# Layer 1 of a two-layer decoder: one pipeline over sequences in place of a loop over groups of four

## What is computed

```python
x = layernorm(x + L0_attn(x)); x = layernorm(x + L0_xattn(x, ctx)); x = layernorm(x + L0_ffn(x))
# layer 1, self-attention: 16 heads of 32, one chunk of 128 tokens
q, k, v = rotary(x @ Wq), rotary(x @ Wk), x @ Wv
y = rms_norm(((q @ k.T) * decay) @ v) @ Wo
x = layernorm(x + y)
# layer 1, cross attention: 8 heads; a token holds 16 features of a head; the 512 columns attend to one another
qk = einsum('bhdq,bhdl->bhql', x, ctx) / sqrt(16)          # 512 x 512 for each head
x = layernorm(x + gamma * einsum('bhql,bhdl->bhdq', softmax(qk), ctx))
x = layernorm(x + experts(x))
```

## Time and profile before

| | us |
|---|---|
| median of three runs (3161.3 to 3161.7) | 3161.61 |
| the profiled execution | 3157.47 |
| its span, first to last instruction | 3155.6 |
| mean granted TensorE clock | 0.925 |

### The profile page before, as it was taken

One profiled execution on the slowest core, in us unless ns is written; L12 is line 12 of the kernel. 1 busy time (PEld: TensorE's weight loads), 2 busy tenths in 40 slices (PEclk: granted clock), 3 DMA queues, 4 the chain that ended last, 5 costly groups with the idle time before them and its releaser, 6 DMA issues. The chain is left out here.

```text
span 3155.6 us, 35463 instructions
## 1 busy us (share of the span) xinstructions
PE 2751.0 (87%) x11005; PEld 1378.1 (44%) x11006; DVE 1416.2 (45%) x2531; ACT 931.9 (30%) x1937; POOL 522.7 (17%) x524
## 2 busy tenths in 40 slices
PE   7999999999998567778778778785989999999998
PEld 3545544554554334224223223223535655566543
DVE  4545635564563522664663673671412222222245
ACT  2334424333433421362362353353001111111101
POOL 2211101110110004102102102200161111111143
PEclk9999999999999778799799799796899999999999
DMA  5121211032121002321321321324012333333244
GB/s 176 54 74 47 80 68 54 28 94 80 54 67 41 1 29 106 96 79 50 102 77 51 100 78 51 98 79 169 9 39 92 129 142 119 124 123 120 64 132 147
DMA packets 96150, 261.90 MB, mean 83 GB/s; under 512 B 19874, under 2 KB 45474, under 8 KB 81922
## 3 DMA queue, kind: packets, MB, share of 16 engines
q1 hardware_dynamic: 81090, 220.87, 20.3%
q0 software_dynamic: 13648, 38.06, 4.2%
q10 hardware_dynamic: 1264, 1.10, 0.1%
HBM read 204.61 MB, written 54.96 MB: 82 GB/s over the span
## 5 line engine op out<-in xcount | busy, mean ns | idle before, releaser
L2397 PE MATMUL d_bank<-d_w,d_xcol 128*128 x1280 | 407.3, 461 | 0.0
L1967 DVE TENSOR_REDUCE c_mx<-c_pair 128x2 f32<-128x1024 f32 x256 | 297.8, 1217 | 88.4 <-PE c_pair L1834 88.2
L1746 ACT ACTIVATE c_area<-c_bank 128x512 f32<-128x512 f32 x512 | 270.2, 615 | 197.0 <-PE c_bank L1847 195.6
L742 PE MATMUL a_bank<-a_xT,a_ring 128*128 128x512 f32 x640 | 286.1, 598 | 10.9 <-DMA a_ident<-in_ident 10.9
L2397 PEld LDWEIGHTS d_bank<-d_w,d_xcol 128*128 128x128 f32 x1280 | 231.8, 191 | 102.4 <-issue 1.5
L507 POOL TENSOR_TENSOR a_ry<-a_rt 128x512 f32<-128x512 f32 x80 | 128.9, 1611 | 800.1 <-DVE a_rt L994 800.1
L1834 PE MATMUL c_pair<-c_ks,c_qs 96*128 96x512 bf16 x512 | 183.6, 461 | 66.4 <-DMA c_qs<-scratch_qpark 30.4
L2404 PE MATMUL d_bank<-d_w,d_hid 128*128 (+1 forms) x486 | 221.9, 592 | 0.7 <-DVE d_hid L2598 0.7
L742 PE MATMUL a_bank<-a_wo,a_ot 128*128 128x512 f32 x512 | 222.4, 592 | 0.0
L1847 PE MATMUL c_bank<-c_qs,c_ks 128*128 128x512 bf16 x512 | 172.0, 406 | 47.6 <-ACT c_area L1746 22.5
L742 PEld LDWEIGHTS a_bank<-a_xT,a_ring 128*128 128x128 f32 x640 | 120.3, 192 | 149.5 <-issue 136.4
(11 more groups left out here) (310 smaller groups left out, 3849.9 us busy)
## 6 DMA issues: line engine op xcount, KB each, us to landing
d_w<-in_w SPq DMA_DIRECT2D x16, 1408.0 KB, 6.7
scratch_results<-d_yrow SPq DMA_DIRECT2D x81, 256.0 KB, 2.0
a_ring<-in_wq SPq DMA_DIRECT2D x16, 1024.0 KB, 4.9
a_wo<-in_wo SPq DMA_DIRECT2D x16, 1024.0 KB, 4.9
c_ks<-scratch_kpark SPq DMA_DIRECT2D x192, 64.0 KB, 2.2
c_qs<-scratch_qpark SPq DMA_DIRECT2D x192, 64.0 KB, 2.2
d_w<-in_w SPq DMA_DIRECT2D x16, 768.0 KB, 8.6
a_ring<-in_w SPq DMA_DIRECT2D x8, 1024.0 KB, 8.4
```

The lines of the kernel that those rows point to most:

```text
L742: ins = pe.matmul(bank[:, :], lhs(c), rhs(c), start=(c == 0), stop=(c == n - 1))
L1746: act.activation(probs[:, n % RING, l, :], bank[:, :], ACT.Exp, scale=float(CD) ** -0.5).then_inc(exped.sem, 1)
L1967: dve.tensor_reduce(mx[:, b % 2, at0:at0 + 2], bank[:, :].rearrange("p (i n) -> p i n", i=2), AX.X, ALU.max).then_inc(maxed.sem, 1)
L2397: ins = pe.matmul(bank[:, 0:FI], xcol[:, v, k, :], w13[:, bass.ds(at, 1), which, k, :].rearrange("p a n -> p (a n)"), start=(k == 0), stop ...
```

## The change

`build_row_fix` is gone as a block; its steps are done in layer 1 behind phase -1 and in phase 0, and the sequences that don't need them go first (`SEQ` puts sequence 0 last). The loop is replaced by straight code of 20 phases. In a phase, stage x2 is a sequence whose exponentials run, x1 the next one, whose maxima run, a2 the one after in the second half of self-attention (scores to output), a1 one more in its first half (projections and turns), and `done` the last one, whose results are added. A phase has 16 slots. In each, TensorE makes two second products, then the small step of that slot, then two or three first products (slots 0 to 12), then in each odd slot a group of values.

- ScalarE takes exponentials of two banks (1024 columns) in one instruction; two such tiles. Scores use the same two.
- VectorE takes maxima of one bank (512 columns); two such banks, 32 instructions for a sequence in place of 16.
- All small steps (projections, turns, attention, squares, output, fix) go through one bank, each waiting until the one before is drained.
- GpSimd makes the pieces of the rows too, and copies the context's rows by sequence; its copy waits for the values of the sequence before last.
- The denominators alone go out and in as 128 x 32, are inverted there and come back spread. Stacks are three sequences deep, each of their six DMAs carries all heads. Loads and stores are by sequence.
- ScalarE loads one table of functions ahead.

SP's order in a phase: loads, sums out, keys, results in, queries, store, maxima. The core of the diff:

```diff
-def build_row_fix(nc, t):
...
-        pair_banks = [ctx.enter_context(nc.psum_tensor(f"c_pair{i}", [P, 1024], F32)) for i in range(2)]
-        banks = [ctx.enter_context(nc.psum_tensor(f"c_bank{i}", [P, 512], F32)) for i in range(3)]
...
+        SEQ = [*range(GB, SEQS), *range(1, GB), 0]
+        one_banks = [ctx.enter_context(nc.psum_tensor(f"c_one{i}", [P, 512], F32)) for i in range(2)]
+        exp_banks = [ctx.enter_context(nc.psum_tensor(f"c_exp{i}", [P, 1024], F32)) for i in range(2)]
+        step_bank = ctx.enter_context(nc.psum_tensor("c_step", [P, 512], F32))
         pv = ctx.enter_context(nc.psum_tensor("c_pv", [P, 512], F32))
...
+        PHASES = range(-3, SEQS + 1)
+        def seq_at(n):
+            return n if 0 <= n < SEQS else None
+        def stages(p):
+            return seq_at(p), seq_at(p + 1), seq_at(p + 2), seq_at(p + 3), seq_at(p - 1)
+        MAX_SLOTS = 13
+        LAST_MAX = MAX_SLOTS - 1
+        def firsts(i):
+            upto = [min(LC * CH, -(-LC * CH * s // MAX_SLOTS)) for s in (i, i + 1)]
+            return range(*upto)
+        SCORES, ATTEND, TURN_X, SQUARES, OUT, V, Q, K, TURN_Q, TURN_K = 0, 2, 3, 4, 5, 7, 9, 11, 13, 14
+        FIX_TURN, FIX_PRODUCT = (-1, 14), (-1, 15)
+        def turn_of(p, i):
+            if i % 2 == 0:
+                return None
+            n, m = (p, (i - 3) // 2) if i >= 3 else (p - 1, TURNS - 1)
+            return (n, m) if seq_at(n) is not None else None
+        one_order, exp_order, step_order = [], [], []
...
+            def load_x(n):
+                if n >= ROWS:
+                    stored.wait(sp, 0, n - ROWS + 1)
+                if n >= 2:
+                    steps.wait(sp, 0, ("xt", n - 2))
+                if SEQ[n] == 0:
+                    fix_out.wait(sp, 0, 1)
+                sp.dma_start(xg[:, n % ROWS, :], seq_rows("x3", n)).then_inc(x_in[n % 2].sem, 16)
+            def load_c(n):
...
+            def load_cT(n):
+                vt_ready.wait(sp, 0, max(n - 1, 0))
+                cols = slice(P * (SEQ[n] % GB), P * (SEQ[n] % GB) + P)
+                sp.dma_start(cT[:, n % 2], t["cT"][SEQ[n] // GB][:, :, cols]).then_inc(cT_in[n % 2].sem, 16)
...
+            def stack(n, ready, part, parked, out, stacked, side, dst):
+                u = n % 2
+                ready.wait(sp, n, 1)
+                stacked[u].wait(sp, n // 2, 0)
+                sp.dma_start(parked[u], part[:, u]).then_inc(out.sem, 16)
+                out.wait(sp, n, 1)
+                if n >= STACKS:
+                    exps.wait(sp, 0, ("e", n - STACKS, LC * CH // 2 - 1))
+                for i, pair in enumerate(TERMS):
+                    sp.dma_start(dst[CD * i:CD * i + CD, n % STACKS],
...
+            def sums_out(n):
+                pv_copied.wait(sp, n, 2)
+                fin_in.wait(sp, n, 0)
+                sp.dma_start(t["ovpark"][n % 2], ov[:]).then_inc(ov_out.sem, 16)
+                ov_out.wait(sp, n, 1)
+                parked = t["ovpark"][n % 2].rearrange("(j e) o n -> e j (o n)", e=32)[CD]
+                sp.dma_start(dn[:, :], parked.rearrange("j (k i) -> j k i", i=32)).then_inc(den_in.sem, 16)
...
+            def results_in(n):
+                inverse.wait(sp, n, 1)
+                sp.dma_start(t["dnpark"][n % 2].rearrange("j (k i) -> (j k) i", i=32), dn[:, :])\
+                  .then_inc(den_out.sem, 16)
+                added.wait(sp, n, 0)
+                parked = t["ovpark"][n % 2].rearrange("(j e) o n -> o j e n", e=32)
+                half = QUAD * CD
+                for o in range(2):
+                    sp.dma_start(fin[half * o:half * (o + 1), 0, :], parked[o, :, 0:CD, :]).then_inc(fin_in.sem, 16)
+                den_out.wait(sp, n, 1)
+                parked = t["dnpark"][n % 2].rearrange("j (o n) -> o j n", o=2)
+                for o in range(2):
+                    sp.dma_start(fin[half * o:half * (o + 1), 1, :],
+                                 parked[o].unsqueeze(1).broadcast_to([QUAD, CD, D])).then_inc(fin_in.sem, 16)
+            def store(n):
+                normed[1].wait(sp, n, 1)
...
+            for p in PHASES:
+                x2, x1, a2, a1, done = stages(p)
+                if seq_at(p + 4) is not None:
+                    load_x(p + 4)
+                if p > -2 and seq_at(p + 3) is not None:
+                    load_c(p + 3)
+                    load_cT(p + 3)
+                if done is not None:
+                    sums_out(done)
+                if a2 is not None:
+                    keys(a2)
+                if done is not None:
+                    results_in(done)
+                if a2 is not None:
+                    queries(a2)
+                if done is not None:
+                    store(done)
+                if p == 0:
+                    fix_step.wait(sp, 0, 5)
+                    sp.dma_start(t["x3"][0][0:E0, 0, :], rows[:]).then_inc(fix_out.sem, 16)
+                if x1 is not None:
+                    maxima(x1)
+            stored.wait(sp, SEQS, 0)
 
...
+            def head_rows(n):
+                cT_in[n % 2].wait(pool, n // 2, 1)
+                if n >= 2:
+                    pv_step.wait(pool, n - 1, 0)
...
+            act.preload_act_table_set("natural_log_exp_and_others")
...
+            def exp_of(n, k):
+                turn = TURNS * n + 2 * k // QUAD
+                if turn >= RING // QUAD:
+                    pv_step.wait(act, 0, turn - RING // QUAD + 1)
+                bank = exps.wait(act, 0, ("e", n, k))
+                at0 = (LC * CH * n + 2 * k) % RING
+                act.activation(probs[:, at0:at0 + 2, :], bank[:, :].rearrange("p (i n) -> p i n", i=2), ACT.Exp,
+                               scale=float(CD) ** -0.5).then_inc(exped.sem, 1)
...
+            def first(n, k):
+                if k == 0:
+                    k_in[n % 2].wait(pe, n // 2 + 1, 0)
+                    q_in[n % 2].wait(pe, n // 2 + 1, 0)
+                h, l = divmod(k, LC)
+                bank = ones_of.start(pe, 0, ("p", n, k))
+                ones_of.done(pe.matmul(bank[:, :], qs[0:TR, n % STACKS, h, l * P:(l + 1) * P],
+                                       ks[0:TR, n % STACKS, h, :], start=True, stop=True))
+            def turn_max(n):
+                bank = ones_of.start(pe, 0, ("mt", n), [at(maxed, n, LC * CH)])
+                ones_of.done(pe.transpose(bank[:, 0:P], mx[:, n % 2, :], ident[:, :]))
+            def second(n, k):
+                if k == 0:
+                    ms_in[n % 2].wait(pe, n // 2 + 1, 0)
+                bank = exps.start(pe, 0, ("e", n, k))
+                for i in range(2):
+                    q, l, j = in_quad(2 * k + i)
+                    h = QUAD * q + j
+                    ins = pe.matmul(bank[:, 512 * i:512 * i + 512], ks[:, n % STACKS, h, l * P:(l + 1) * P],
+                                    qs[:, n % STACKS, h, :], start=True, stop=True)
...
+            def values(n, m):
+                q, l = divmod(m, LC)
+                exped.wait(pe, n, QUAD * (m + 1) // 2)
+                vt_ready.wait(pe, n, 1)
+                if l == 0:
+                    pv_copied.wait(pe, n, q)
+                for j in range(QUAD):
+                    ins = pe.matmul(pv[32 * j:32 * j + 32, :], head_values(n, q, l, j),
+                                    probs[:, (LC * CH * n + QUAD * m + j) % RING, :],
+                                    start=(l == 0), stop=(l == LC - 1))
+                ins.then_inc(pv_step.sem, 1)
...
+            for p in PHASES:
+                x2, x1, a2, a1, done = stages(p)
+                for i in range(SLOTS):
+                    if x2 is not None:
+                        second(x2, i)
+                    if a2 is not None and i == SCORES:
+                        scores(a2)
+                    if a2 is not None and i == ATTEND:
...
+            def maximum(n, k):
+                bank = ones_of.wait(dve, 0, ("p", n, k))
+                dve.tensor_reduce(mx[:, n % 2, k:k + 1], bank[:, :], AX.X, ALU.max).then_inc(maxed.sem, 1)
...
+            def invert(n):
+                den_in.wait(dve, n, 1)
+                dve.reciprocal(dn[:, :], dn[:, :]).then_inc(inverse.sem, 1)
+            def finish(n):
+                row = xg[:, n % ROWS, :]
+                fin_in.wait(dve, n, 4)
+                chained(dve.scalar_tensor_tensor(fin[:, 0, :], fin[:, 0, :], gamma[:, 0:1], fin[:, 1, :],
+                                                 ALU.mult, ALU.mult))
+                dve.tensor_tensor(row, row, fin[:, 0, :], ALU.add).then_inc(added.sem, 1)
...
+            for p in PHASES:
+                x2, x1, a2, a1, done = stages(p)
+                for i in range(SLOTS):
+                    if a2 is not None and i == SCORES:
+                        mask(a2)
+                    if a2 is not None and i == ATTEND:
+                        scale_out(a2)
+                    if done is not None and i == 4:
+                        invert(done)
```

(2 more changed lines are left out.)

975 lines of the change are left out of this document (407 added, 568 removed).

## The result

The changed kernel takes 3197.39 us (median of four runs, 3193.44 to 3202.64) against 3161.45 for the kernel before: ratio 1.0121, 95% interval 1.0108 to 1.0133. The forecast was 3194. Its profiled execution took 3193.44 us.

The account below looks back on a forecast made before the run. TensorE's 40 us a phase is the floor, but waits make 56.7, weight loads 58.5, clock falls 62.5; 24 + 102 + 59 + 750 + 119 = 1054 us against 1021.4, so 3194, 8-in-10 range 3105 to 3250.

Parts of the forecast that it names:

- The walk: Slot-by-slot timing of one layer 1 phase at full clock: 56.7 us, TensorE idle 17 of it.
- A: The forecast itself: engines wait in turn and the clock falls, phase 60.3 to 64.5 us, 3167 to 3220; chance 0.45.
- alternation's weight loads: TensorE's weight-load cost of alternation in a phase, 8 x 0.23 us, adding 1.8 us: 58.5.
- The term of the clock: Half of six TensorE idle stretches a phase make its clock fall, about 1.6 us each; 4 us taken.
- Rival E: Clock falls in all six idle stretches of a phase: phase 66.5 us, 3250; chance 0.06.
- Rival B: The clock holds: phase 56.7 to 58.5 us, shorter fill and drain, 3118; chance 0.33.
- The chain of results: SP's DMAs in order, ending in loads for the finish step: 28.7 us, hidden with 2.8 us to spare.
- Rival C: SP's order makes the finish step start at 35 to 36 us: phase 66.5 us, 3250; chance 0.09.
- rival D: ScalarE's one table isn't kept, Ln and Exp still load in turn, 6 loads a phase: 3220; chance 0.07.

Follow-up runs that it names:

- hand-out run: Kernel with all edits together and shortened fill (0.964), only its first products again handed out evenly, two or three per slot 0 to 12: ratio 0.9848 to the kernel before.
- filler run: Changed kernel plus eight matmuls without a reader, filling TensorE's idle time in slot 0 ahead of the third first product: ratio 1.0088 to the kernel before.
- interleaving: Changed kernel with first products issued between a projection's four matmuls instead of behind them: ratio 1.0106 to the kernel before.
- half projections: Changed kernel with V, Q and K taking two of their four matmuls, so results differ: ratio 0.9986 to the kernel before.
- section 5: Two parts alone in the kernel before: maxima split into two 512-column instructions, ratio 1.007; ScalarE's one table loaded ahead of layer 1's loop, ratio 1.0009.

## Why the prediction was right, point by point

**The mechanism.** The walk holds. From the phase's start at 1782.32 the measured slots 1 to 13 begin at 6.9, 10.2, 14.6, 17.0, 19.8, 25.2, 28.2, 33.4, 37.3, 42.6, 45.6, 50.8 and 53.7 us; the walk had 6.3, 8.4, 12.5, 14.7, 17.5, 22.7, 25.9, 31.1, 35.0, 40.2, 43.4, 48.6 and 51.9. The difference grows to 1.8 us in slots 1 and 2, where the clock falls, and from there to slot 13 stays between 1.8 and 2.5. TensorE's six stretches of idle time for a maximum (2.50, 1.57, 1.50, 2.61, 1.51, 1.65) and VectorE's of about 3 us in four projections are in the places named. But the walk had each of the six longer (2.7, 2.0, 2.1, 2.85, 2.1, 2.2), and it didn't have TensorE's 0.79 us in slot 4, behind a reciprocal that waits for its load. (The waits that it names add up to 15.7 us and not to 17; the slots' times don't hang on that sum.) The hand-out run shows that this alternation is a cause: 5.0 us a phase, some 4 of them at full clock.

**The phase, 62.5 forecast, 60.4 measured.** That is the lower edge of A's 60.3 to 64.5. The full-clock phase is 57.5 to 58.0 by the filler run's undisturbed phases, between the walk's 56.7 and the 58.5 with alternation's weight loads. The term of the clock, 4 us, was mis-sized in the count, not in the price. Windows of the kernel after, two neighbouring phases, then of the first of them what follows the idle stretch of slot 0, and the rest:

```profile
1784.19:1843.35 59.16, 44.10 (x241) 16.64 (x246) 32.88 (x59) 21.20 (x29) 12.99 (x14) 0.94 0.34 77
1843.35:1903.61 60.26, 45.00 (x241) 17.10 (x246) 32.78 (x59) 21.20 (x29) 12.98 (x14) 0.94 0.34 76
1788.00:1794.00 6.00, 5.38 (x34) 1.40 (x39) 2.91 (x5) 1.98 (x3) 1.25 (x4) 0.54 0.00 0
1796.19:1841.00 44.81, 35.53 (x157) 13.61 (x160) 26.48 (x51) 16.90 (x24) 11.52 (x10) 1.00 0.40 88
```

Some 7 us of nearly every phase run at the half rate: in one phase as one fall (1786.6 to 1793.4), in the next as two of 3.4 us (from 1848 and from 1879). I had three. The phase with one is 59.2 us, 1.5 above the 57.7 without a fall, near the 1.6 that I worked out from the earlier trace rows; the phase with two is 2.6 above. The count was off for a reason that the trace shows: I had six idle stretches of 2.0 to 2.85 us and let half of them make the clock fall, but only two are over 2 us, slot 0's of 2.50 and slot 8's of 2.61. Of the twenty falls that begin in phases 1 to 12 eleven come at slot 0's, seven at slot 8's and two at shorter ones; none comes in slots 6, 10 or 12. Rival E, every stretch, is out, and with it the plain form of the Trainium skill's rule ("TensorE: Matmul & The Clock Gate", A second HAM failure mode: psum-queue depth-cycling): small idle times did make the clock go up and down here, but in most phases at one or two of six stretches. Rival B, no fall, is what five of the filler run's phases show; the kernel after has no such phase among its twelve.

**The sum, 1054 forecast, 1060 measured.** It came out right because two errors cancel. The twelve phases are 725 us, not 750. Constants (24.5), phases -3 and -2 (20.7, 35.2), phase 0 (58.3) and the last results (21.8) are as forecast. Phase -1 took 60.0 us, not 47: its maxima are over at 1287.35, 48 us after its start, and then the fix's turn and product stand alone on TensorE, the product at half clock (TensorE's timeline; at full clock eight such matmuls take 3.60). I had named it and not priced it:

```profile
1292.63 6.61 PE L1881 MATMUL c_step<-c_probs 128*128 128x512 f32 x8 [0.78 <-DVE c_probs L1999]
```

The drain's three phases took 49.4, 37.2 and 27.8, not 46, 33 and 18. The last is the results' chain again: ScalarE's exponentials stand behind the root of the second norm, which waits for the finish step, which waits for its loads. VectorE and TensorE there (ScalarE's root starts at 2188.83):

```profile
2186.25 0.75 DVE L1964 SCALAR_TENSOR_TENSOR c_fin<-c_fin,c_gamma 128x512 f32<-128x512 f32 x1 [8.50 <-DMA c_fin<-scratch_dnpark]
2190.32 1.95 PE L1824 MATMUL c_exp<-c_qs,c_ks 128*128 128x512 bf16 x4 [8.07 <-ACT c_probs L1671]
```

So 25 us too much in the middle and 30 too little at the ends. The forecast's 3194 owes its nearness to luck there; and it gave "slower" no more than 0.54.

**The chain of results.** I gave it 28.7 us against 31.5 for the finish step; the step starts at 33.5 in the phase shown, and in none of the phases 1 to 12 does it wait for its loads (its three waits, 18.5 us, are in the drain). So the chain was hidden, as forecast, but it was longer than 28.7: the cT load goes out at 11.9 us into the phase, not at 8.5, since it waits for values of slot 1, which the fall delays, and the last of the four loads is only issued by 28.4. Rival C took effect as soon as interleaving, or half projections, made anything faster.

**Prices.** Groups by line of the kernel after, layer 1 (busy us, mean ns of one, idle before):

```profile
L1944 DVE TENSOR_REDUCE c_mx<-c_one 128x1 f32<-128x512 f32 x512 | 323.7, 680 | 228.7 <-PE c_one L1810 226.9
L1671 ACT ACTIVATE c_probs<-c_exp 128x1024 f32<-128x1024 f32 x256 | 260.8, 1023 | 447.6 <-PE c_exp L1824 425.8 <-remote 21.2 <-issue 0.3
L1810 PE MATMUL c_one<-c_ks,c_qs 96*128 96x512 bf16 x512 | 177.4, 408 | 165.0 <-DVE c_mx L1944 164.7
```

Maxima 0.68 and exponentials 1.02 us, as forecast; 256 double exponentials are busy for 260.8 us where 512 single ones took 4 x 67.5 = 270, so two banks at once save 3% on an engine that waits 448 us in the layer. VectorE's 32.9 us a phase against 34, TensorE's waits 165 us. Table loads are gone (rival D out), and section 5 shows that they were worth nothing.

## What to carry to other kernels

When two engines hand banks to each other in order, put the long work of one into the same slot as the long work of the other, and cut a long group of matmuls open so that the other's food comes out during it; adding up busy times doesn't show this, walking one period slot by slot does. Before paying for a faster step, look at the chain that is hidden with 2 or 3 us to spare, because it is the next bound. And where TensorE waits in many short stretches, its clock is part of the sum: judge an edit by its phases at full clock and by how many phases keep it, separately.
